# A selective scan's prologue: bias by a one-row product, relu and sum in one VectorE operation, a row copy on ScalarE, and the second drive ahead of a subtraction

## The reference, cut to what matters

```python
xc = silu(conv(x_in) + conv_b)
sel = einsum('ble,se->bls', xc, sel_w)
dt_in, Bm, Cm = sel[..., :16], sel[..., 16:32], sel[..., 32:]
dt = softplus(einsum('blr,er->ble', dt_in, dt_w) + dt_b)
dA = exp(dt[..., None] * A)
dBu = dt[..., None] * Bm[:, :, None, :] * xc[..., None]
h = dA_t * h + dBu_t            # over the 1024 positions, 16 states
y = einsum('ben,bn->be', h, C_t)
```

## Time and profile before

| | |
|---|---|
| median of 3 runs | 1472.17 us (1472.07 to 1472.51) |
| the profiled execution's own time | 1474.32 us |
| its span | 1472.5 us |
| PE busy | 1267.6 us, 86% |
| DVE busy | 1009.3 us, 69% |
| ACT busy | 596.9 us, 41% |
| POOL busy | 471.9 us, 32% |
| mean granted clock of TensorE | 0.946 of 2.4 GHz |

### The profile page before, as it was taken

The page is one execution under the profiler, slowest core; times in us unless marked ns, Lnnn a source line. Parts: engine busy times, 40 slices in busy tenths (PEclk is TensorE's granted clock), DMA queues, the critical chain, the costliest instruction groups (busy, mean ns, idle before and its releaser), DMA issues.

```text
span 1472.5 us, 16490 instructions
## 1 busy us (share of the span) xinstructions
PE 1267.6 (86%) x5746; PEld 541.6 (37%) x5746; DVE 1009.3 (69%) x1106; ACT 596.9 (41%) x823; POOL 471.9 (32%) x254
## 2 busy tenths in 40 slices
PE   6957789989985779998997678999899687899988
PEld 2213333337422233324732223333573232333265
DVE  2489965675559895667555989566746599856683
ACT  0263443425244434333525433533451644343345
POOL 3249920012006990002100898000210099700040
PEclk9979999999997999999998899999999889999998
DMA  8333412230013440232001343022100134312310
GB/s 236 113 131 136 152 56 68 90 76 1 15 38 109 157 155 17 84 94 58 1 15 52 123 152 135 23 92 93 41 1 15 61 129 169 102 33 83 90 30 15
DMA packets 58929, 119.33 MB, mean 81 GB/s; under 512 B 9922, under 2 KB 27106, under 8 KB 58338
## 3 DMA queue, kind: packets, MB, share of 16 engines
q1 hardware_dynamic: 58242, 113.95, 23.7%
q10 hardware_dynamic: 608, 4.34, 1.0%
HBM read 113.00 MB, written 5.26 MB: 80 GB/s over the span
## 4 chain that ended last, share of the span: by engine, by line
PE 58%; DVE 13%; POOL 11%; ACT 8%; issue 6%; DMA 3%; SPq 1%; POOLq 0%; DVEq 0%; ACTq 0%
PE ps L708 9%; PE ps L685 8%; PE ps L700 8%; POOL scratch L487 7%; DVE scratch L1208 6%; PE ps L637 4%; PE ps L568 4%; PE ps L554 4%; DVE scratch L1197 3%; PE ps L813 3%; PE ps L615 2%; PE ps L865 2%; PE ps L581 2%; DMA decayT<-in_decayT 2%; POOL scratch L501 2%
## 5 line engine op out<-in xcount | busy, mean ns | idle before, releaser
L487 POOL TENSOR_TENSOR scratch<-scratch 128x1024 f32<-128x1024 f32 x124 | 291.2, 2366 | 337.2 <-DVE scratch L1208 337.2
L637 PE MATMUL ps<-scratch,consts 128*128 128x512 f32 x512 | 257.7, 637 | 15.5 <-POOL scratch L487 15.3
L501 POOL TENSOR_TENSOR scratch<-scratch,rmax 128x1024 f32<-128x1024 f32 x32 | 61.5, 1923 | 570.0 <-DVE rmax L1319 570.0
L1208 DVE TENSOR_TENSOR_SCAN scratch<-ps,scratch 128x1024 f32<-128x1024 f32 x100 | 225.5, 2278 | 0.5
L976 ACT ACTIVATE ps<-steps,vec 128x1024 f32<-128x1024 f32 x128 | 143.0, 1117 | 196.1 <-DVE scratch L1208 194.1
L1244 DVE TENSOR_TENSOR scratch<-scratch,ps 128x1024 f32<-128x1024 f32 x108 | 131.9, 1221 | 113.0 <-issue 76.2
L615 PE MATMUL ps<-bc,pick 128*128 128x512 bf16 x256 | 86.5, 423 | 121.2 <-DVE scratch L1197 78.3
L1022 ACT ACTIVATE scratch<-ps 128x1024 f32<-128x1024 f32 x108 | 108.8, 1023 | 163.6 <-PE ps L685 163.6
L637 PEld LDWEIGHTS ps<-scratch,consts 128*128 128x128 f32 x512 | 101.6, 204 | 135.9 <-issue 91.9
L1197 DVE TENSOR_TENSOR scratch<-steps,ps 128x1024 f32<-128x1024 f32 x100 | 122.1, 1221 | 36.9 <-PE ps L615 30.5
L685 PE MATMUL ps<-h_odd,w 64*128 64x512 f32 x512 | 141.8, 640 | 3.8 <-ACT scratch L1022 3.8
(11 more groups left out here) (202 smaller groups left out, 1634.5 us busy)
## 6 DMA issues: line engine op xcount, KB each, us to landing
scratch<-c_rows SPq DMA_DIRECT2D x128, 512.0 KB, 3.7
xc<-gate_rows SPq DMA_DIRECT2D x96, 128.0 KB, 2.9
zs<-gate_rows SPq DMA_DIRECT2D x96, 128.0 KB, 3.0
steps<-routed_table SPq DMA_DIRECT2D x128, 64.5 KB, 1.9
decayT<-in_decayT SPq DMA_DIRECT2D x8, 512.0 KB, 17.6
work<-in_table ACTq DMA_DIRECT2D x1, 2064.0 KB, 15.5
routed_table<-work SPq DMA_DIRECT2D x1, 2064.0 KB, 6.3
w<-in_w ACTq DMA_DIRECT2D x4, 512.0 KB, 21.9
```

Of the source, the lines that this page charges most:

```text
L487: pool.tensor_tensor(hc_slot(k), hs_slot(k), c_slot(k), ALU.mult).then_inc(sem["hc_ready"], 1)
L637: m = mm(ps[:, 6 + c, :], ident, hc_slot(k)[:, c * CH:(c + 1) * CH], start=(n == 0), stop=(n == NS - 1))
L1208: dve.tensor_tensor_scan(hs_slot(k), banks(dA_bank(k)), dbu_slot(k), 0.0, ALU.mult, ALU.add).then_inc(sem["scanned"], 1)
```

## The change

The edits are these. The bias dt_b of g = 0 is no longer added by ACT but by PE: the row dt_b (1 x 128, a new part of the constant tile `rows`, which grows from 80 to 208 columns) times a row of ones, two products with one row and 512 columns, accumulated in banks 2 and 3. ACT's relu for g = 0 goes; DVE takes max(x, 0) + ln in one operation that reads x from PSUM. The copy of the rows of C for g = 0 moves from DVE to ACT, behind the logarithm. The first spread waits for that copy in place of `dt_read`. Drive 1 stands ahead of `sel_rest(1)`.

```diff
+        dt_b_row = rows[0:1, NX + WS:NX + WS + E]
...
                     for c in range(NC):
                         m = mm(ps[:, DT_BANK[g] + c, :], w_dt[:, :], xc[:, g, c * CH:(c + 1) * CH],
-                               start=True, stop=True)
+                               start=True, stop=bool(g))
+                    if g == 0:
+                        for c in range(NC):
+                            m = mm(ps[:, DT_BANK[g] + c, :], dt_b_row, v("one")[0:1].to_broadcast([1, CH]),
+                                   start=False, stop=True)
                     m.then_inc(sem["dt_ps"], 1)
...
-                    pe.wait_ge(sem["dt_read"], at(pair, "dt_read", 1))
+                    pe.wait_ge(sem["c_rows"], at(pair, "c_rows", 1))
...
                 def dt_size(g):
-                    act.activation(dt_neg(g), banks(DT_BANK[g]), ACT.Abs, bias=v("dt_b")).then_inc(sem["dt_read"], 1)
+                    act.activation(dt_neg(g), banks(DT_BANK[g]), ACT.Abs,
+                                   bias=v("dt_b") if g else 0.0).then_inc(sem["dt_read"], 1)
...
                 first_parts(0)
-                dt_above(0)
+                act.wait_ge(sem["dt_ps"], at(pair, "dt_ps", 1))
                 dt_size(0)
                 exp_dt(0)
                 log_dt(0)
+                act.activation(c_rows(0), banks(SEL_BANK[0])[0:32], ACT.Copy).then_inc(sem["c_rows"], 1)
                 first_parts(1)
...
-                dve.wait_ge(sem["sel_hi"], at(pair, "sel_hi", 1))
-                dve.tensor_copy(c_rows(0), banks(SEL_BANK[0])[0:32]).then_inc(sem["c_rows"], 1)
                 sel_rest(0)
...
-                dve.tensor_tensor(dt[:, 0, :], dt_pos(0), dt_neg(0), ALU.add).then_inc(sem["dt_ready"], 1)
+                dve.scalar_tensor_tensor(out=dt[:, 0, :], in0=banks(DT_BANK[0]), scalar=0.0, in1=dt_neg(0),
+                                         op0=ALU.max, op1=ALU.add).then_inc(sem["dt_ready"], 1)
...
                 drive(0)
                 scan(0)
+                drive(1)
                 sel_rest(1)
-                drive(1)
...
     rows = _np.concatenate([
         _np.broadcast_to(a["L0_ffn_gate_b"], (P, NX)),
-        _np.concatenate([windows, windows])], axis=1)
+        _np.concatenate([windows, windows]),
+        _np.broadcast_to(a["L0_attn_dt_b"].reshape(1, E), (P, E))], axis=1)
```

## The result

| | before | changed |
|---|---|---|
| median of 17 runs, taken side by side | 1472.51 us | 1470.34 us |
| lowest and highest | 1471.34, 1476.33 | 1461.53, 1476.57 |
| the profiled execution's own time, span | 1474.32, 1472.5 | 1464.89, 1463.1 |

The ratio is 0.9973, 95% interval 0.9960 to 0.9986. The forecast, 1470.4 us, lies 0.1 us from the median; that closeness is luck, since the interval alone is 3.8 us wide. Later the same changed kernel was measured again at 0.9981 (0.9958 to 1.0004). What has to be explained is less the median than the spread: the changed kernel's times cover 15 us, and its profiled execution is 9.4 us shorter than that of before, where my path gives 1.7. The spread is not its own, though: the kernel before covered 5.0 us in these 17 runs, and 9.4 (17 runs), 15.9 (35 runs) and 6.1 us (12 runs) beside the experiments.

The account below looks back on a forecast made before the run. The prologue's PE, ACT, DVE chain was taken to bound the changed stretch; +0.72 - 1.15 = -0.43 us per pair, -1.7 over four, from 1472.17 gives 1470.4 us, chance 0.48, range 1466.9 to 1474.0.

Parts of the forecast that it names:

- Where the path runs: Each pair's prologue: chain goes from PE's step-size product through ACT's relu, abs, logarithm to DVE's sum, u, drive 0, scan 0.
- The one-row products: PE, between the step-size product and abs, once per pair: two products of 512 columns together take 1.73 us.
- The ends of 1.06 and 3.46: Lowest and highest us for the two one-row products: 64-row products side by side, or twice 1.73; -4.4 or +5.2 in all.
- both rivals on them: One-row products cheap at 1.06, 1467.8 us, chance 0.09; or dear at 3.46, 1477.4 us, 0.07 shared with a late spread.
- The relu that goes, and the operation that takes its place: ACT ahead of abs, 1.73 - 1.01 = +0.72 us per pair; DVE's combined relu and sum, +0.00.
- The row copy: C's rows copied by ACT behind the logarithm: worth nothing; first spread keeps 0.5 us cover at worst, POOL starts 0.5 late.
- The order: Drive 1 ahead of the subtraction of g = 1: scan 0 to scan 1 from 7.13 to 5.98 us, gain 1.15 per pair.
- The larger constant tile: Load among the first small tiles, 64 KB more: costs nothing, at most 0.3 us once.
- The signs of a right forecast: Products 1.7, abs 1.75 behind L598, logarithm-scan 0 5.03, scan 0-scan 1 5.9-6.0, no DVE idle, POOL DMA-released, PEclk 0.50.
- One sign of a wrong forecast: Stages far from the prologue change length by some 3 us, with DVE's work the same and PEclk different.
- The sum: Prologue shift and order together: +0.72 - 1.15 = -0.43 us per pair, -1.7 us over four pairs.
- The clock: Attention's granted clock, 3.1 us a stage: in favour 0.25 (1467.4 us); one stage lost 0.06 (1473.6), two 0.05 (1476.7).

## Why the prediction was right, point by point

**Where the path runs**. Right: in the traces of both kernels the chain went PE, ACT, DVE as read, and a microsecond taken from it in the run without the bias products came back whole (1.91 of 1.93).

**The one-row products.** Predicted 1.73, measured 1.93. The mis-sized term of the sum: it is the seam between one row and 128, +0.2 per pair; with 128 rows it was 1.74. The ends of 1.06 and 3.46 were far off, and both rivals on them fell. That these products are a pure loss in place of ACT's relu was right.

**The relu that goes, and the operation that takes its place.** Predicted shift 0.72, measured 0.82 to 0.84: +0.2 from the seam, and -0.07 from abs to exp, 1.06 (432.25 to 433.31) where it was 1.13 (435.07 to 436.20). Abs with a constant as bias took 1.02 in every trace that has it, with a bias from a tile 1.09 to 1.12; the sum had no term for this. Relu and sum in one took 1.22, so +0.00 was right.

**The row copy.** Right: nothing, on either engine. The cover of the first spread was 0.9 us, where 0.5 at worst was forecast. POOL was released by a load, 1.04 late and not 0.5, at no cost.

**The order.** Predicted 1.15, measured 1.31. Most of the difference is drive 1, 2.20 behind scan 0 and not 2.32, while the intervals around the subtraction stayed at 1.23 and 1.26. With the old order put back, the subtraction started 2.32 behind scan 0 again. This agrees with the rule of the Trainium skill, page "VectorE: DVE Perf Modes", section "Two Vector instructions with no wait between them", which the prediction named and did not put into its sum.

**The larger constant tile.** Right: nothing to be seen. The kernel's first product starts at 9.58 to 9.73 us in the three traces with the small tile and at 9.64 to 9.74 in the nine with the large one.

**The signs.** The signs of a right forecast came, three of them with other sizes: the products 1.93 and not 1.7, abs 1.95 and not 1.75 behind the end of L599, scan 0 to scan 1 5.82 and not 5.9 to 6.0. Behind scan 0 the granted clock stood at 0.50 from 440.8 to 454.5. One sign of a wrong forecast came as well: stages far from the prologue changed by some 3 us with DVE's work the same, once in favour (pair 2's attention) and once against (pair 1's).

**The sum.** Predicted -0.43 per pair, -1.7 us; measured 0.82 - 1.31 = -0.49, -2.0 us. That the two agree is partly luck: the shift was 0.10 dearer and the order 0.16 better than forecast, and the two misses nearly cancel. The medians differ by 2.2 us, the ratios of the two measurements by 4.0 and 2.8 us with intervals that reach down to 2.1 and to nothing. Whether the change wins something beyond its path on average was not settled; with single runs 15 us apart it would take many more.

**The clock.** It was a rival with 0.25 in favour and 0.11 against, placed in the attention stage at 3.1 us a piece. Both the place and the price hold (3.2 us), but the clock works in more places than I gave it: the start, beside the loads of the decay mask, steps 4 and 5 (scan 1 to scan 5 took 13.9 to 14.5 us), steps 16 to 19, and attention, where in these two traces nothing was won (one long stage each, pair 2 before, pair 1 after). I took the narrow spread of three runs, 0.4 us, for a property of the kernel; the kernel before then spread over 5 to 16 us, the changed one over 15 and 17.

## What to carry to other kernels

Price an operation that is moved between engines by where it stands: TensorE was busy 86% and ScalarE 41%, and both work of the one and of the other was on the path here, while VectorE, waiting 2.41 us at the same point, took the relu and left the prologue 1.05 shorter. When two executions differ in parts that share no code with the change, compare stage by stage, and count the change by the starts inside its own stretch, where 0.02 us can be told, before the whole time, where 10 us of a single execution cannot. Three executions within 0.4 us do not show that a kernel's time is steady. A loop whose rounds are equally long can meet the same clock in every round, as in the one trace with 358.40 us a round, and then an average over few runs says little.

## What the runs showed that was not expected

- One kernel's times fell into two groups, 1459.6 to 1462.0 and 1473.1 to 1480.7 us, with the granted clock lower in every execution of the second. With 1.8 us more work on the path, on another chip, they did not.
- A VectorE sum of 128x1024 took 1.38 us, in all eight cases, when it started 0.3 us before the end of POOL's operation on 32x1024, and 1.23 otherwise; the relu with a scalar from a tile took 1.28 both with and without POOL beside it. Why was not tested.
- The first 70 us vary by 3.6 between traces. A part goes with when the decay mask lands: the same VectorE product waited for its load until 37.12 in the trace of before and 35.13 in that of the changed kernel, and from 37 to 44 us the granted clock was 0.51 in the one and 1.00 in the other.
